# Tokenizer, state-space scan and expert layer on one core: taps, token means and expert products of the last stage issued at other steps

## The chip, the cores and the metric

One core of one Trainium2 chip runs the whole program. Times are device microseconds (us) of one execution; the time of a kernel is the median of its runs. About 0.2% (18 us) is what a measurement of this kernel can tell from no change.

## What is computed

A batch of 4 images (3 x 224 x 224) goes through two "performer" blocks that make tokens, and a projection makes 3136 tokens of 768 channels each. Then comes one layer: a state-space scan and a routed expert layer, each on a normalised input and added to it.

```python
t = _unfold3(t, 2).transpose(0, 2, 1)
h = t @ proj_w.T + proj_b                         # 3x3 taps, stride 2, of 64 channels
x = layernorm(h)
Bproj, Cproj = x @ W_B + b_B, x @ W_C + b_C       # 16 each
delta = softplus(x @ W_D + b_D + p_Delta)
state = exp(delta * A) * state + B_bar * x        # 768 x 16 states, token by token
h = h + sum_n(C[n] * state[n])
x = layernorm(h)
route = argmax(softmax((x @ enc_w + enc_b) @ sw_w + sw_b))          # one of 8 experts
h = h + prob * (gelu(x @ w1[route] + b1[route]) @ w2[route] + b2[route])
```

## The kernel before

Three stages follow each other: `performer1`, `performer2` and `tail`. Only `tail`, the last, is touched; it takes the span from about 3600 us on.

**Units and steps.** `tail` works on 28 units (`UNITS`) of 448 tokens (`T`; 4 images of 7 units). A unit has 24 steps (`STEPS`), one for each pair of a chunk of 128 channels (`dc`, 6 of them) and a group of 4 of the 16 states (`q`). In a step GpSimd (POOL) multiplies h by B (`weigh_in`, line 1482), ScalarE (ACT) makes four decays in PSUM (`step`, line 1762), VectorE (DVE) weighs with them (`weigh`, line 1871; four) and scans (`scan`, line 1880; two), GpSimd multiplies the states by C (`weigh_out`, line 1494, two steps later), and TensorE (PE) sums the states into bank YB (`step`, line 1573). After every fourth step an identity product adds h (line 1577), and ScalarE writes the result back to h (`add_to_h`, line 1751) one full step group later: at steps 3 (of the unit before), 7, 11, 15, 19 and 23. The v buffers form a ring of 6.

**Side work.** Between the steps stand two other chains. `front(i + 1, k)` makes the next unit's h and its B, C and delta: the taps, six products of 128 channels (lines 1532 and 1534, here PJ0 to PJ5), each moved out by ScalarE (line 1688, HW0 to HW5) before the next may start, since all use bank BF; a seventh tap product for the token means (MU, written by line 1691); sums of squares in two parts (VAR0, VAR1, line 1523); Ln and Exp of the variance (lines 1700 and 1702); the B and C product (BC) and the delta product (Z), both line 1527; and on VectorE the writes of B and C (lines 1852 to 1855), Z (1846) and delta (1861). `mlp(i - 1, k)` is the expert layer of the unit before: squares (SQ0, SQ1) and mean (MEAN) on TensorE, the encoder product (ENC), four expert products (IN0 to IN3, line 1527, each moved from bank BS by VectorE in line 1924 before the next may start), the route logits (LOG), the turned route (TURN, line 1609, copied by VectorE in line 1951, here OH), four masks (lines 1622 and 1957), and eight outputs (OUT0 to OUT7, lines 1635 to 1638), two banks in turn, each moved by ScalarE (line 1796).

**Order.** Every engine runs its own list in order: for step k of loop i first its part of the step, then `mlp(i - 1, k)`, then `front(i + 1, k)`. The steps at which each piece is issued are tuples of constants (from line 1330): P_ for TensorE, A_ for ScalarE, V_ for VectorE. The number in the tuple is a step of that engine's own list, and the engines are not at the same step at the same time: at every fourth step TensorE waits for an h write that stands in ScalarE's list three steps later (lines 1565 and 1751). The SyncE queue issues the loads and the spreads (lines 1346 to 1467); the token load of unit i + 2 (line 1358) waits until the seven tap products of unit i + 1 are done, the load of `w2` (line 1451) for IN3.

Of the kernel before, what the change touches and what calls it, by code (L numbers as in the profile page):

```python
# [42 lines left out]
def after(eng, s, count):  # L43

    if count > 0:
        eng.wait_ge(s, count)
# [1110 lines left out]
STEPS = Q * DC  # L1157
UNITS = B * J3
# [18 lines left out]
def tail(nc, sem, w, c, t2, w1c, xd, dd, bcd, out):  # L1177

    with ExitStack() as ctx:
# [5 lines left out]
        def bank(k, n=T, rows=slice(0, 128)):  # L1185
            return ps[rows, k, 0:n]
# [140 lines left out]
        s_oa = sem("t_out_written")  # L1327
        s_out = [sem("t_out_stored_even"), sem("t_out_stored_odd")]

        P_PJ, P_MU, P_VAR, P_Z, P_BC = 1, 7, (8, 10), 11, 9  # L1330
        A_HW, A_MU, A_SQ, A_RS, A_MX, A_SP = 5, 11, (9, 13), 14, (16, 17), (17, 18)
        V_Z, V_BC, V_DL = 15, 14, (18, 19)
        P_SQ, P_MEAN, P_ENC, P_IN, P_LOG, P_TURN = (0, 2), 1, 4, 5, 6, 10
        P_MASK, P_OUT = (12, 13, 14, 15), (16, 17, 18, 18, 19, 20, 21, 22)
        A_SQ2, A_MS, A_RS2, A_EX, A_GL = (2, 4), 5, 7, 11, 14
        A_OUT = (21, 22, 23, 23, 24, 25, 26, 27)
        V_VAR, V_ENC, V_IN, V_LOG, V_EQ, V_OH, V_MASK = 6, 8, 9, 10, 12, 14, (16, 17, 18, 19)
        ROUTE, TAIL = 9, 28

        def means(i):  # L1340

# [175 lines left out]
        def _(pe):  # L1517
            mm = nc.tensor.matmul

            def squares_sum(i, ln, into, chunks):  # L1520
                for dc in chunks:
                    pe.wait_ge(s_sq[ln], DC * i + dc + 1)
                    mm(into, jm[:, :], sq[:, dc % 3, :], start=(dc == 0), stop=(dc == DC - 1)).then_inc(s_var[ln], 1)  # L1523

            def over_chunks(into, weights, i):
                for dc in range(DC):
                    last = mm(into, weights(dc), h[:, i % 3, dc, :], start=(dc == 0), stop=(dc == DC - 1))  # L1527
                return last

            def taps(into, even, odd):  # L1530
                for j in range(3):
                    mm(into, even(j), x3[:, 0:TR3, j:j + 2 * S3 - 1:2], start=(j == 0), stop=False)  # L1532
                for j in range(3):
                    last = mm(into, odd(j), x3[0:64, 1:TR3 + 1, j:j + 2 * S3 - 1:2], start=False, stop=(j == 2))  # L1534
                last.then_inc(s_pj, 1)

            def front(i, k):
                if P_PJ <= k < P_PJ + DC:
                    dc = k - P_PJ
                    cols = slice(128 * dc, 128 * dc + 128)  # L1540
                    if dc == 0:
                        pe.wait_ge(s_x, 32 * (i + 1))
                        after(pe, s_dl, DC * i)
                    else:
                        pe.wait_ge(s_hw, DC * i + dc)
                    taps(bank(BF), lambda j: wpa[:, j, cols], lambda j: wpj[:, j, cols])
                if k == P_MU:
                    pe.wait_ge(s_hw, DC * (i + 1))
                    taps(ps[few, BF, 0:T], lambda j: wma[:, j, :], lambda j: wmb[:, j, :])
                if k == P_VAR[0]:  # L1550
                    pe.wait_ge(s_mu, i + 1)
                    squares_sum(i, 0, bank(BF), range(0, 3))
                if k == P_VAR[1]:
                    squares_sum(i, 0, bank(BF), range(3, DC))
                if k == P_Z:
                    pe.wait_ge(s_ln[0], i + 1)
                    over_chunks(bank(BF), lambda dc: wz[:, dc, :], i).then_inc(s_z, 1)
                if k == P_BC:
                    after(pe, s_he, MT * (i - 1))
                    over_chunks(ps[0:48, BS, 0:T], lambda dc: wbc[:, dc, :], i).then_inc(s_bc, 1)  # L1560

            def step(i, k):

                dc, q = divmod(k, Q)
                n = STEPS * i + k
                if q == 0:
                    after(pe, s_hy, DC * i + dc)
                if k in OWN:
                    pe.wait_ge(s_cv, 2 * owned(n))
                else:  # L1570
                    pe.wait_ge(s_cm, others(n))
                for g in range(4):
                    last = mm(ps[32 * g:32 * g + 32, YB, 0:T], dg[:, 4 * k + g, :], v[:, n % RING, g, 1:T + 1],  # L1573
                              start=(q == 0), stop=False)
                last.then_inc(s_ns, 1)
                if q == Q - 1:
                    mm(bank(YB), ident[:, :], h[:, i % 3, dc, :], start=False, stop=True).then_inc(s_hs, 1)  # L1577
# [74 lines left out]
            last.then_inc(s_pm, 1)  # L1652
            pe.wait_ge(s_dgm, 1)
            pe.wait_ge(s_pd, 16)
            for k in range(STEPS):
                front(0, k)
            for i in range(UNITS + 1):
                for k in range(TAIL if i == UNITS else STEPS):
                    if i < UNITS:
                        step(i, k)  # L1660
                    if i >= 2 and k + STEPS < TAIL:
                        mlp(i - 2, k + STEPS)
                    if i >= 1:
                        mlp(i - 1, k)
                    if i + 1 < UNITS:
                        front(i + 1, k)

        @block.scalar
        def _(act):
# [95 lines left out]
            def mlp(i, k):  # L1765
# [23 lines left out]
                for o in range(2 * NCH):  # L1789
                    if A_OUT[o] != k:  # L1790
                        continue
# [214 lines left out]
def build(nc, w, c, out):  # L2006
    t1 = nc.dram_tensor("tokens1", (B, E, T1ROWS, IMG), F32, kind="Internal").ap()
    t2 = nc.dram_tensor("tokens2", (B, E, T2ROWS, S2), F32, kind="Internal").ap()
    w1c = nc.dram_tensor("centred_w1", (128, DC, NX * NR), F32, kind="Internal").ap()
    xd = nc.dram_tensor("h_by_channel", (2, DC, 32, 4, T), F32, kind="Internal").ap()  # L2010
    dd = nc.dram_tensor("delta_by_channel", (2, DC, 32, 4, T), F32, kind="Internal").ap()
    bcd = nc.dram_tensor("bc_rows", (2, 2, N, T), F32, kind="Internal").ap()
    stages = (lambda sem: performer1(nc, sem, w["x"], w, c, t1),
              lambda sem: performer2(nc, sem, w, c, t1, t2),
              lambda sem: tail(nc, sem, w, c, t2, w1c, xd, dd, bcd, out))
    for stage in stages:
        sems = []

        def sem(name):
            sems.append(nc.alloc_semaphore(name))  # L2020
            return sems[-1]

        stage(sem)
        nc.clear_and_free_semaphores(sems)
        nc.all_engine_barrier()
# [133 lines left out]
```

## Time and profile before

| | before |
|---|---|
| median of 3 runs | 9070.57 us (9055.2 to 9074.09) |
| the profiled execution | 9071.86 us |
| its span, first to last instruction | 9070.1 us |
| mean granted TensorE clock | 0.916 |
| busy PE / DVE / ACT / POOL | 85% / 68% / 47% / 66% of the span |
| steps x units in the last stage | 24 x 28 |

The profile shows one execution. Busy shares are over all three stages; in the last stage POOL and DVE are busy nearly all the time. A row of a timeline gives start, duration, engine, line, operation, operands and count, and in brackets how long the engine had been idle and who released it. A duration of merged instructions runs from the first start to the last end; matmul ends are modelled, so the work of a piece is best read from one start to the next.

### The profile page before, as it was taken

How to read it: one execution, taken by the hardware profiler on the slowest of the kernel's cores; microseconds unless marked ns; L12 is line 12 of the kernel's file. 1: busy time of each engine (PE TensorE's matmuls, PEld its weight loads, DVE VectorE, ACT ScalarE, POOL GpSimd, SP SyncE). 2: the span in 40 equal slices, each digit the busy share in tenths (PEclk: the TensorE clock that was granted, in tenths of full speed). 3: DMA queues.
4: the chain of work that ended last, by engine and by line, in shares of the span. 5: the costliest groups of instructions: out<-in, count | busy, mean ns of one | idle time of the engine just before them, and what ended most of it. 6: DMA issues, size and time to landing. Idle time of an engine off the chain costs nothing.

```text
span 9070.1 us, 86859 instructions
## 1 busy us (share of the span) xinstructions
PE 7693.1 (85%) x31228; PEld 3214.3 (35%) x31228; DVE 6124.9 (68%) x6499; ACT 4306.6 (47%) x7641; POOL 5969.4 (66%) x2484
## 2 busy tenths in 40 slices
PE   6799999776999996588788888788887888888887
PEld 3444444322444432133333333333333333333333
DVE  1355555442233333988888888888888888888885
ACT  1366666553344432445544445444445444454442
POOL 0011111115766640998999989999989999899995
PEclk9999999998999997799889998899988899988988
DMA  0011111114544432223233223333232332233331
GB/s 26 22 41 45 39 44 41 31 31 83 104 100 100 99 65 68 95 98 119 96 120 115 100 96 119 106 112 116 94 119 96 123 112 100 99 116 106 117 110 50
DMA packets 356855, 786.60 MB, mean 87 GB/s; under 512 B 70437, under 2 KB 282806, under 8 KB 348936
## 3 DMA queue, kind: packets, MB, share of 16 engines
q1 hardware_dynamic: 320376, 690.75, 25.0%
q0 software_dynamic: 21712, 51.75, 2.2%
q10 hardware_dynamic: 14336, 38.54, 1.2%
q8 instruction: 247, 4.05, 0.2%
q14 instruction: 184, 1.51, 0.1%
HBM read 597.36 MB, written 183.35 MB: 86 GB/s over the span
## 4 chain that ended last, share of the span: by engine, by line
PE 34%; DVE 14%; ACT 5%; issue 5%; POOL 2%; DMA 0%; SPq 0%; DVEq 0%; ACTq 0%; POOLq 0%
PE ps L1527 7%; DVE v L1880 6%; PE ps L1635 6%; DVE v L1871 6%; PE ps L1534 5%; PE ps L1532 5%; PE ps L1573 3%; ACT ps L1762 3%; PE ps L1523 2%; PE ps L1638 2%; PE ps L1636 2%; PE ps L1577 1%; POOL v L1482 1%; POOL v L1494 1%; DVE dl L1861 1%
## 5 line engine op out<-in xcount | busy, mean ns | idle before, releaser
L1880 DVE TENSOR_TENSOR_SCAN v<-ps,v 128x898 f32<-128x898 f32 x1344 | 2725.5, 2028 | 92.4
L1494 POOL TENSOR_TENSOR v<-v,ct 128x1792 f32<-128x1792 f32 x672 | 2473.8, 3681 | 447.6 <-ACT st L1723 447.6
L1482 POOL TENSOR_TENSOR v<-xr,bt 128x1792 f32<-128x1792 f32 x672 | 2472.8, 3680 | 97.3 <-DMA xr<-h_by_channel 97.3
L1762 ACT ACTIVATE ps<-dr,aa 128x448 f32<-128x448 f32 x2688 | 1585.6, 627 | 1526.7 <-DVE v L1880 1509.5
L1871 DVE SCALAR_TENSOR_TENSOR v<-ps,aa,v 128x448 f32<-128x448 f32 x2688 | 1690.5, 671 | 553.6 <-ACT ps L1762 527.1
L222 POOL DMA_DIRECT2D tokens<-ob x448 | 235.4, 532 | 1878.2 <-ACT ob L383 1827.4
L1635 PE MATMUL ps<-w_or_w,gm 128*112 128x384 f32 x1792 | 719.9, 551 | 370.1 <-DVE gm L1957 277.5
L1573 PE MATMUL ps<-v,dg 128*32 128x448 f32 x5376 | 705.8, 599 | 206.9 <-POOL v L1494 106.3
L1635 PEld LDWEIGHTS ps<-w_or_w,gm 128*112 128x112 f32 x1792 | 334.0, 197 | 768.7 <-DVE gm L1957 319.9
L1527 PE MATMUL ps<-h,w_or_w 128*128 128x448 f32 x1344 | 536.8, 549 | 16.3 <-DVE gm L1924 16.3
L1532 PE MATMUL ps<-x,wpa 128*128 128x448 f32 x1008 | 445.3, 577 | 17.2 <-ACT h L1688 10.2
L1688 ACT ACTIVATE h<-ps,pbias 128x448 f32<-128x448 f32 x168 | 106.4, 633 | 732.7 <-PE ps L1534 732.7
L1534 PE MATMUL ps<-x,wpb 64*128 64x448 f32 x1008 | 448.3, 576 | 0.0
L498 DVE COPY ht<-ps 112x512 f32<-112x512 f32 x112 | 77.5, 692 | 546.6 <-ACT kp L411 546.6
L812 PE MATMUL ps<-xt,wa 128*64 128x448 f32 x2016 | 434.5, 564 | 0.0
L1523 PE MATMUL ps<-sq,jm 128*128 128x448 f32 x672 | 315.5, 611 | 61.5 <-ACT ot L1796 56.8
L1527 PEld LDWEIGHTS ps<-h,w_or_w 128*128 128x128 f32 x1344 | 250.3, 191 | 298.6 <-issue 279.2
L471 DVE RECIPROCAL qpn<-qpn 128x448 f32<-128x448 f32 x112 | 330.7, 2953 | 3.8
L1573 PEld LDWEIGHTS ps<-v,dg 128*32 128x32 f32 x5376 | 110.0, 112 | 611.2 <-issue 284.7
L1622 PE MATMUL ps<-wpb 9*128 9x448 f32 x224 | 151.8, 768 | 194.8 <-DVE gm L1957 194.1
L1118 DVE TENSOR_TENSOR kq<-ps,rsa 128x896 f32<-128x896 f32 x56 | 61.1, 1092 | 358.2 <-PE ps L820 336.9
L276 PE MATMUL ps<-wki,h 128*112 128x256 f32 x896 | 282.0, 398 | 21.3 <-DVE hu L493 21.3
(324 smaller groups left out, 11919.9 us busy)
## 6 DMA issues: line engine op xcount, KB each, us to landing
xr<-h_by_channel SPq DMA_DIRECT2D x168, 896.0 KB, 7.3
dr<-delta_by_channel SPq DMA_DIRECT2D x168, 896.0 KB, 6.3
x<-tokens SPq DMA_DIRECT2D x252, 224.0 KB, 5.3
tokens<-ob POOLq DMA_DIRECT2D x448, 112.0 KB, 2.4
w_or_w<-in_w SPq DMA_DIRECT2D x29, 1536.0 KB, 6.4
w_or_w<-centred_w SPq DMA_DIRECT2D x27, 1536.0 KB, 6.4
h_by_channel<-h SPq DMA_DIRECT2D x112, 336.0 KB, 10.9
delta_by_channel<-dl SPq DMA_DIRECT2D x112, 336.0 KB, 4.8
```

The source lines that it names most:

```text
L812: mm(ps[half[g], o, 0:T], wa[:, j, cols], xt[:, 2 * (n % 3) + g, 0:TR2, j:j + 2 * S2 - 1:2], start=(j == 0), stop=False)
L1482: tt(v[:, n % RING, :, 1:T + 1], xr[:, dc % 2, 1:].rearrange("p (i t) -> p i t", i=4), bt[:, q:q + 1, :].to_broadcast([128, 4, T]), ALU.mu ...
L1494: tt(v[:, n % RING, :, 1:T + 1], v[:, n % RING, :, 1:T + 1], ct[:, q:q + 1, :].to_broadcast([128, 4, T]), ALU.mult).then_inc(s_cm, 1)
L1523: mm(into, jm[:, :], sq[:, dc % 3, :], start=(dc == 0), stop=(dc == DC - 1)).then_inc(s_var[ln], 1)
L1527: last = mm(into, weights(dc), h[:, i % 3, dc, :], start=(dc == 0), stop=(dc == DC - 1))
L1532: mm(into, even(j), x3[:, 0:TR3, j:j + 2 * S3 - 1:2], start=(j == 0), stop=False)
L1534: last = mm(into, odd(j), x3[0:64, 1:TR3 + 1, j:j + 2 * S3 - 1:2], start=False, stop=(j == 2))
L1573: last = mm(ps[32 * g:32 * g + 32, YB, 0:T], dg[:, 4 * k + g, :], v[:, n % RING, g, 1:T + 1], start=(q == 0), stop=False)
L1635: mm(into[:, 0:D // 2], gm[:, m, cs], w2[:, m, lo:lo + D // 2], start=(m == 0), stop=False)
L1762: fn(decay(g), dr[:, dc % 2, g, :], ACT.Exp, scale=aa[:, 4 * k + g:4 * k + g + 1]).then_inc(s_a, 1)
L1871: stt(row, decay(g), aa[:, 4 * k + g:4 * k + g + 1], row, ALU.subtract, ALU.mult).then_inc(s_wt, 1)
L1880: nc.vector.tensor_tensor_scan(row, flat[:, 1024 * pair:1024 * pair + 2 * T + 2], row, 0.0, ALU.mult, ALU.add).then_inc(s_sc, 1)
```

## The change

The constants change, and TensorE's loops call the taps of a unit two steps before the first step of the loop in which they stood. P_PJ goes from 1 to -2: PJ0 and PJ1 are issued at steps 22 and 23 of the loop before, PJ2 to PJ5 at steps 0 to 3. ScalarE's HW0 to HW5 go from steps 5 to 10 to steps 2 to 7. MU, the squares, BC, the expert products, TURN's copy, the masks and the last outputs move by one or two steps. The last loop has 27 steps instead of 28 (`TAIL`). No instruction is added or removed.

```diff
-        P_PJ, P_MU, P_VAR, P_Z, P_BC = 1, 7, (8, 10), 11, 9
-        A_HW, A_MU, A_SQ, A_RS, A_MX, A_SP = 5, 11, (9, 13), 14, (16, 17), (17, 18)
+        P_PJ, P_MU, P_VAR, P_Z, P_BC = -2, 5, (7, 9), 11, 10
+        A_HW, A_MU, A_SQ, A_RS, A_MX, A_SP = 2, 9, (7, 11), 13, (16, 17), (17, 18)
         V_Z, V_BC, V_DL = 15, 14, (18, 19)
-        P_SQ, P_MEAN, P_ENC, P_IN, P_LOG, P_TURN = (0, 2), 1, 4, 5, 6, 10
-        P_MASK, P_OUT = (12, 13, 14, 15), (16, 17, 18, 18, 19, 20, 21, 22)
+        P_SQ, P_MEAN, P_ENC, P_IN, P_LOG, P_TURN = (0, 2), 1, 4, 6, 6, 10
+        P_MASK, P_OUT = (11, 12, 13, 14), (16, 17, 18, 18, 19, 20, 20, 21)
         A_SQ2, A_MS, A_RS2, A_EX, A_GL = (2, 4), 5, 7, 11, 14
-        A_OUT = (21, 22, 23, 23, 24, 25, 26, 27)
-        V_VAR, V_ENC, V_IN, V_LOG, V_EQ, V_OH, V_MASK = 6, 8, 9, 10, 12, 14, (16, 17, 18, 19)
-        ROUTE, TAIL = 9, 28
+        A_OUT = (21, 22, 23, 23, 24, 25, 25, 26)
+        V_VAR, V_ENC, V_IN, V_LOG, V_EQ, V_OH, V_MASK = 6, 8, 10, 10, 12, 13, (15, 16, 17, 18)
+        ROUTE, TAIL = 9, 27
...
-            for k in range(STEPS):
+            for k in range(P_PJ, STEPS):
                 front(0, k)
+            for k in range(P_PJ, 0):
+                front(1, k)
             for i in range(UNITS + 1):
                 for k in range(TAIL if i == UNITS else STEPS):
...
                     if i + 1 < UNITS:
                         front(i + 1, k)
+                    if i + 2 < UNITS and k >= STEPS + P_PJ:
+                        front(i + 2, k - STEPS)
```

## Rows read from the trace of the kernel before

**Rows 1.** The page's costliest groups: GpSimd's work on the states.

```profile
L1494 POOL TENSOR_TENSOR v<-v,ct 128x1792 f32<-128x1792 f32 x672 | 2473.8, 3681 | 447.6 <-ACT st L1723 447.6
```

**Rows 2.** Who waited for whom, 4000 to 8900 us: total, times, longest.

```profile
ACT h L1688 <- PE ps L1534: 667.8, 140, 7.5
DVE v L1871 <- ACT ps L1762: 504.8, 160, 4.8
POOL v L1494 <- ACT st L1723: 425.3, 201, 5.0
```

**Rows 3.** Timeline of DVE, 6700 to 6800 us: its waits at steps 7, 9 to 12, 14.

```profile
6727.62 1.27 DVE L1871 SCALAR_TENSOR_TENSOR v<-ps,aa,v 128x448 f32<-128x448 f32 x2 [2.93 <-ACT ps L1762]
...
6743.44 1.28 DVE L1871 SCALAR_TENSOR_TENSOR v<-ps,aa,v 128x448 f32<-128x448 f32 x2 [2.00 <-ACT ps L1762]
...
6755.44 1.28 DVE L1871 SCALAR_TENSOR_TENSOR v<-ps,aa,v 128x448 f32<-128x448 f32 x2 [4.84 <-ACT ps L1762]
...
6767.46 1.28 DVE L1871 SCALAR_TENSOR_TENSOR v<-ps,aa,v 128x448 f32<-128x448 f32 x2 [4.30 <-ACT ps L1762]
...
6777.18 1.28 DVE L1871 SCALAR_TENSOR_TENSOR v<-ps,aa,v 128x448 f32<-128x448 f32 x2 [2.56 <-ACT ps L1762]
...
6799.45 0.62 DVE L1852 TENSOR_TENSOR ps<-ps,rs 48x448 f32<-48x448 f32 x1 [0.42 <-ACT rs L1702]
```

**Rows 4.** Timeline of PE, OUT4 of one unit to MU of the next.

```profile
6673.22 2.83 PE L1635 MATMUL ps<-w_or_w,gm 128*112 128x384 f32 x8 [3.43 <-ACT ot L1796]
...
6677.65 0.96 PE L1573 MATMUL ps<-v,dg 128*32 128x448 f32 x8
...
6682.97 0.96 PE L1573 MATMUL ps<-v,dg 128*32 128x448 f32 x8
...
6699.66 4.85 PE L1523 MATMUL ps<-sq,jm 128*128 128x448 f32 x6 [2.56 <-ACT ot L1796]
...
6715.51 0.96 PE L1573 MATMUL ps<-v,dg 128*32 128x448 f32 x8
...
6723.85 0.96 PE L1573 MATMUL ps<-v,dg 128*32 128x448 f32 x8
...
6725.59 2.56 PE L1532 MATMUL ps<-x,wpa 128*128 128x448 f32 x6
...
6730.68 0.96 PE L1573 MATMUL ps<-v,dg 128*32 128x448 f32 x8
...
6741.42 0.96 PE L1573 MATMUL ps<-v,dg 128*32 128x448 f32 x8
...
6752.02 0.96 PE L1573 MATMUL ps<-v,dg 128*32 128x448 f32 x8
...
6775.03 0.96 PE L1573 MATMUL ps<-v,dg 128*32 128x448 f32 x8
```

**Rows 5.** Timeline of PE further on: TURN, Z after an idle stretch, the next OUT4.

```profile
6789.82 0.93 PE L1609 MATMUL ps<-ident,eq 112*9 112x112 f32 x8
...
6798.86 7.52 PE L1527 MATMUL ps<-h,wz 128*128 128x448 f32 x12 [3.82 <-ACT rs L1700]
...
6865.09 4.53 PE L1635 MATMUL ps<-w_or_w,gm 128*112 128x384 f32 x8 [3.43 <-ACT ot L1796]
...
6871.22 0.96 PE L1573 MATMUL ps<-v,dg 128*32 128x448 f32 x8
```

**Rows 6.** Timeline of ACT, 6700 to 6800 us: HW4 and its wait.

```profile
6752.13 0.63 ACT L1688 ACTIVATE h<-ps,pbias 128x448 f32<-128x448 f32 x1 [7.54 <-PE ps L1534]
```

**Rows 7.** Timeline of DVE: the first scans of steps 21 and 22.

```profile
6848.28 2.03 DVE L1880 TENSOR_TENSOR_SCAN v<-ps,v 128x898 f32<-128x898 f32 x1
...
6854.81 2.03 DVE L1880 TENSOR_TENSOR_SCAN v<-ps,v 128x898 f32<-128x898 f32 x1
```

**Rows 8.** Groups of DVE instructions, 3900 to 8900 us: the moves of IN0 to IN3.

```profile
L1924 DVE TENSOR_TENSOR gm<-ps,rs2t 128x448 f32<-128x448 f32 x105 | 63.0, 600 | 1.2 <-PE ps L1527 1.2
```

**Rows 9.** Stretch of Z: busy time and count of PE, PEld, DVE, ACT, POOL; clock, DMA.

```profile
6798.90:6806.30 7.40, 7.40 (x12) 3.31 (x12) 6.74 (x10) 4.67 (x11) 5.91 (x3) 0.63 0.37 132
```

## The prediction

> **What bounds the kernel now.** I read the costliest groups first. GpSimd's two products are 3.68 us each, two a step and 24 steps, so 176.7 us of work a unit, and it is idle only because ScalarE's copy of the last states is late [rows 1]. The table of waits says who makes it late: GpSimd waits for ScalarE, ScalarE's h writes (HW) wait for TensorE's taps, and VectorE then waits for ScalarE's decays [rows 2]. The timeline of VectorE shows where in a unit: 2.93 us at step 7, 2.00, 4.84, 4.30 and 2.56 at steps 9 to 12 [rows 3]. It never waits for GpSimd in this unit, so it is VectorE's work plus these waits that make the unit's length.
>
> The timeline of TensorE gives the cycle that closes on itself. One period runs from OUT4 (released by ScalarE) at 6673.22 to the next OUT4 at 6865.09, 191.87 us [rows 4, 5]. It has three parts: (a) TensorE's row of pieces from OUT4 to the end of MU at 6775.03, 101.81 us, nearly without idle time; (b) from there by ScalarE to VectorE's step 12 at 6777.18 [rows 3], 2.15 us; (c) VectorE's steps 12 to 22 and the hand-over to OUT4, 87.91 us. In (a) ScalarE's in-order list keeps VectorE at TensorE's pace. So the change must be judged by where TensorE's row ends and how many steps VectorE then still has to do.
>
> **Part (a), after.** The last piece that ScalarE waits for is now PJ5, issued at step 3 and moved out at step 7; MU, at step 5, is wanted only at ScalarE's step 9. From starts to next starts in [rows 4]: an output 4.43; a step's sum and an output 5.32, so a sum 0.89; a sum with the identity product 1.74; a tap product 5.09; sum, squares and taps 8.34; sum, twelve matmuls of a full product and taps 10.60. The new row is
> - OUT4 4.43, sum and OUT5 5.32, OUT6 4.43, sum and OUT7 5.32: 19.50;
> - step 22: sum and PJ0, 5.98; step 23: sum, identity, PJ1, 6.83;
> - step 0: SQ0 and PJ2, 8.34; step 1: MEAN and PJ3, 10.60; step 2: SQ1 and PJ4, 8.34; step 3: sum, identity, PJ5, 6.83.
>
> That is 66.42 us. OUT4 follows 3.43 us of idle time, and the second OUT4 took 6.13 to its next start, 1.70 more [rows 5]; I take this for every unit, so 68.1. Against 101.81, 33.7 go: ENC, three IN, LOG, MU and the sums of four steps, and with them SQ0's 2.56 us wait for ScalarE's last output move [rows 4], because OUT7 now comes ahead of the taps.
>
> The price is seen inside the row: the identity product of step 23, which ScalarE needs for its h write at step 3 before any decay, now stands behind PJ0. So VectorE gets a new wait at step 3, and others at 5, 6 and 7. They are not added: TensorE's row holds them all.
>
> **Part (b), after.** The h write of PJ5 is followed by three squares, as HW4 is now: TensorE done at 6752.02, VectorE going on at 6755.44 [rows 3, 4, 6], 3.4 us, 1.3 more than MU's.
>
> **Part (c), after.** It starts at step 8 instead of 12. Four steps of 6.53 (6848.28 to 6854.81) [rows 7] are 26.1. The side work of VectorE that moves into this part is ENC, LOG's three small operations and a net three of the IN moves: five pieces of about 0.6 each [rows 8], 3.0. The rest of the side work is the same, a step earlier or later; it is never on a path of its own.
>
> The IN chain becomes a round trip: TensorE is now on time, so IN1 waits for VectorE's move of IN0 at step 10, after some 4 us of idle time. From that move TensorE does IN1 4.62, VAR0 2.36, twice a sum with a product 5.51, VAR1 2.36, a sum 0.89 and TURN 0.86 (6789.82 to the next piece, estimated from its 0.93) [rows 4, 5], 22.1 us. VectorE does three steps 19.6, three IN moves 1.8, LOG 0.6 and the route's small operations, estimated at 1.1: 23.1. Then it wants TURN for OH, at step 13 now and not 14. At the full clock that is no wait. But Z, after 3.82 us idle, took 7.52 us where such a product takes 4.6, with a mean granted clock of 0.63 in its stretch, between the levels of 1.2 and 2.4 GHz [rows 5, 9]. The same after IN1's idle time adds 1.7 (OUT4's excess) to 2.9 (Z's). I take 2.3, so OH waits 1.3 us; the ends are 0.7 and 1.9. ScalarE's Ln waits for VAR1 too and adds 0.2 behind it; the 0.42 us wait at step 14 [rows 3] goes, since Ln and Exp are now a step earlier.
>
> By a rule of the Trainium skill it would be worse. "TensorE: Matmul & The Clock Gate", Part 1, says that back-to-back matmuls at the lower clock start twice as far apart. Were IN1 so throughout, it would add 4.6 and not 2.3; the trace has 2.9 at most. This is a rival below.
>
> **Costed at nothing.** Masks and OUT0, OUT1 come one step earlier, but OUT2 and OUT3 wait for ScalarE's moves of steps 21 and 22, so the wait at step 23 stays. BC goes behind TURN, hidden before VectorE's step 14. The eighth output's move at step 2 waits for OUT7 on ScalarE, and so do its squares and HW0; VectorE feels it only through the same h write at step 3. On the SyncE queue the token load comes earlier and is not needed for 12 steps; `w2` waits for IN3, a step later, and holds back the spread for chunk 4, with a few us left before GpSimd wants it and a ring of 6 behind that. GpSimd, at 176.7 us, has room under 189. The last loop's missing step holds no work.
>
> **The sum.** 68.1 + 3.4 + 87.9 + 26.1 + 3.0 + 1.3 + 0.2 - 0.4 = 189.6 against 191.87: 2.3 us less a unit. Loops 1 to 26 have both chains: 26 x 2.3 = 60. The profiled execution took 9071.86; 9012, and the median is 1.3 under that execution: **9011 us**. It is the difference of two large numbers, 33.7 off TensorE's row and 31 put back elsewhere, so an error of 2 us in either moves the total by 52.
>
> **Rivals.**
> - *The waits simply go.* If the taps, being early, held nobody up, the five waits, 16.6 us a unit, would vanish, down to GpSimd's 176.7: 26 x 15.2 = 395 less, 8675. For it: these waits are by name the taps'. Against it: TensorE's row has no idle time in it to give. 5%.
> - *The row stays warm.* If neither OUT4 nor IN1 meets the lower clock, 1.7 + 1.3 more go, 5.3 a unit: 8933. For it: TensorE is busier ahead of OUT4 in some units (6673.22 was at full clock). 14%.
> - *Nothing gained.* IN1 wholly at the lower clock: OH waits 3.6 instead of 1.3, which eats the 2.3: 9071. 14%.
> - *Slower.* Place: step 13, OH behind TURN. If the lower clock lasts over IN1 and VAR0, it adds 7.0, OH waits 6.0, 4.7 more than I took: 2.4 a unit lost, 26 times, 9133. It decides from an excess of 4.6 us. For it: a new gap, new lower-clock work on the path, and VAR0 directly behind. Against it: in none of the rows did it last so long under load. 22%.
>
> That the change does not do what it says is not in doubt: constants and calls match.
>
> **How the numbers follow.** My case has 45%. The range, 8930 to 9135, reaches from the warm row to the slower rival; outside it are the first rival and a part of the last. A measurement of this kernel can tell about 0.2%, 18 us, from no change. Faster: 45 + 5 + 14 = 64%; same 14%; slower 22%.
>
> **What would show it.** VectorE's waits at steps 9 to 12 gone, new ones at step 3 (4 to 6 us) and 5 to 7 (some 8 together); step 23's wait still near 4; TensorE's row from OUT4 to PJ5's end at 66 to 69; IN1 released by line 1924 after idle time; a wait of VectorE of 1 to 2 us at line 1951 or its step. GpSimd idle near 13 a unit. I am wrong if the row is longer than 71, if OH waits over 3.6, or if VectorE waits for GpSimd's line 1482.

## The result and the profile after

| | before, beside it | after |
|---|---|---|
| median | 9070.36 us (4 runs) | 9103.71 us (4 runs, 9094.68 to 9111.47) |
| ratio, 95% interval | | 1.003 [1.0017, 1.0042] |
| the profiled execution, its span | 9071.86, 9070.1 us | 9098.96, 9097.2 us |
| mean granted clock | 0.916 | 0.911 |

The change makes the kernel slower, by 33 us in the medians and by 0.3% in the ratio, more than the 0.2% that a measurement can tell. The forecast was 9011 us, faster; its range, 8930 to 9135, held the result. Now and then an execution of any of these kernels takes far longer (12353.83 us in one of the four of pjm1), and such executions are left out of the ratios and of pjm1's median.

VectorE after, from step 3 of a unit to step 23, in the timeline (start, duration, engine, line, operation, count, idle time before and releaser). Line numbers of ScalarE and VectorE are 4 higher than before, those of TensorE up to 1638 the same: the weighing is L1875 now, the move of an expert product L1928, the copy of the route L1955.

```profile
6727.76 1.28 DVE L1875 SCALAR_TENSOR_TENSOR v<-ps,aa,v 128x448 f32<-128x448 f32 x2 [6.66 <-ACT ps L1766]
...
6741.19 1.28 DVE L1875 SCALAR_TENSOR_TENSOR v<-ps,aa,v 128x448 f32<-128x448 f32 x2 [0.26 <-ACT ps L1766]
...
6751.79 1.28 DVE L1875 SCALAR_TENSOR_TENSOR v<-ps,aa,v 128x448 f32<-128x448 f32 x2 [3.96 <-ACT ps L1766]
...
6761.88 1.28 DVE L1875 SCALAR_TENSOR_TENSOR v<-ps,aa,v 128x448 f32<-128x448 f32 x2 [2.93 <-ACT ps L1766]
...
6768.43 1.25 DVE L1875 SCALAR_TENSOR_TENSOR v<-ps,aa,v 128x448 f32<-128x448 f32 x2
...
6788.82 0.60 DVE L1928 TENSOR_TENSOR gm<-ps,rs2t 128x448 f32<-128x448 f32 x1
...
6800.54 1.28 DVE L1875 SCALAR_TENSOR_TENSOR v<-ps,aa,v 128x448 f32<-128x448 f32 x2 [3.50 <-ACT ps L1766]
...
6817.95 0.62 DVE L1955 TENSOR_TENSOR wpb<-ps,mu 9x448 f32<-9x448 f32 x1 [2.24 <-PE ps L1609]
6818.82 1.28 DVE L1875 SCALAR_TENSOR_TENSOR v<-ps,aa,v 128x448 f32<-128x448 f32 x2 [0.24 <-ACT ps L1766]
...
6889.42 1.28 DVE L1875 SCALAR_TENSOR_TENSOR v<-ps,aa,v 128x448 f32<-128x448 f32 x2 [3.45 <-ACT ps L1766]
```

The waits of [rows 3] at steps 9, 10 and 11 are gone. New ones stand at steps 3, 5, 6 and 7 (6.66, 0.26, 3.96, 2.93), and the one at step 23 stayed (3.45): all these were forecast. The row without a bracket, 6768.43, is the first weighing of step 8. What was not forecast is the wait of 3.50 us **at step 12**, and the 2.24 at step 13 is larger than the 1.3 I had put there.

TensorE in the same unit:

```profile
6695.84 5.46 PE L1635 MATMUL ps<-w_or_w,gm 128*112 128x384 f32 x8 [3.43 <-ACT ot L1800]
...
6764.94 0.96 PE L1573 MATMUL ps<-v,dg 128*32 128x448 f32 x8
...
6783.63 1.02 PE L1577 MATMUL ps<-h,ident 128*128 128x448 f32 x2
6789.47 6.86 PE L1527 MATMUL ps<-h,w_or_w 128*128 128x448 f32 x12 [4.83 <-DVE gm L1928]
6796.17 2.42 PE L1523 MATMUL ps<-sq,jm 128*128 128x448 f32 x6
...
6807.74 6.26 PE L1527 MATMUL ps<-h,w_or_w 128*128 128x448 f32 x12 [2.67 <-DVE gm L1928]
...
6890.99 2.83 PE L1635 MATMUL ps<-w_or_w,gm 128*112 128x384 f32 x8 [3.43 <-ACT ot L1800]
```

The row from OUT4 (6695.84) to PJ5's end (6764.94) is 69.10 us long; in [rows 4] the row to MU's end was 101.81. IN1 (6789.47) waits for VectorE's move of IN0, and VAR0 (6796.17) stands behind it. IN3 (6807.74) waits in the same way for the move of IN2, at VectorE's step 12, and VAR1 and TURN stand behind it. ScalarE shows who stands behind VAR0: the second squares of the front, L1684, and later Ln, L1704, behind VAR1.

```profile
6797.18 0.58 ACT L1684 ACTIVATE sq<-h 128x448 f32<-128x448 f32 x1 [6.84 <-PE ps L1523]
...
6816.30 0.63 ACT L1704 ACTIVATE rs<-ps,eps 128x448 f32<-128x448 f32 x1 [7.76 <-PE ps L1523]
```

The table of waits of after, 4000 to 8900 us (total, times, longest), says that this happens in each of the 25 units of the stretch:

```profile
DVE v L1875 <- ACT ps L1766: 502.3, 187, 7.0
ACT h L1692 <- PE ps L1534: 458.5, 150, 5.3
POOL v L1494 <- ACT st L1727: 451.0, 222, 4.4
...
ACT rs L1704 <- PE ps L1523: 176.2, 25, 7.8
ACT sq L1684 <- PE ps L1523: 172.6, 75, 6.8
```

Against [rows 2], ScalarE waits less for the taps (667.8 before, 458.5 now), VectorE as long for ScalarE (504.8, 502.3), GpSimd longer (425.3, 451.0). The last two rows are waits that [rows 2] do not show.

**The sum, redone with this unit.** Unit length is 6890.99 - 6695.84 = 195.15. Part (a) 69.10, forecast 68.1. Part (b), 6764.94 to 6768.43, 3.49, forecast 3.4. Part (c), 6768.43 to 6890.99, 122.56; forecast 87.9 + 26.1 + 3.0 + 1.3 + 0.2 - 0.4 = 118.1. The 4.46 that are over in (c) are the wait at step 12 (3.50) and 0.98 more at step 13 and behind it (2.24 + 0.24 against 1.3 + 0.2): 4.48. The sum needs nothing else; what stands behind the 2.24 is taken up with the reasons below.

In the next unit OUT4 met the full clock, and that unit took 190.55: 2.77 less in (a), waits of 2.89 and 0.76 in place of 3.50 and 2.24. The units go on in that beat, and the mean of the 26 units that have both chains, from VectorE's first weighing of one to that of the next, is 192.8 (before 191.8, by the same count). The forecast 189.6 plus the mean wait at step 12, 3.2, is 192.8.

### The profile page after: what moved, and what is told of

The parts are those of the page before. It is cut to its first block, busy times and chain, and to the rows that moved or that the text cites. A ratio compares the mean times of both kernels' runs of the same rounds, so it can differ in the third digit from the quotient of the medians.

```text
span 9097.2 us, 86859 instructions
## 1 busy us (share of the span) xinstructions
PE 7754.3 (85%) x31228; PEld 3257.6 (36%) x31228; DVE 6124.5 (67%) x6499; ACT 4320.2 (47%) x7641; POOL 5968.6 (66%) x2484
## 4 chain that ended last, share of the span: by engine, by line
PE 28%; DVE 19%; issue 7%; ACT 4%; POOL 3%; DMA 0%; SPq 0%; DVEq 0%; ACTq 0%; POOLq 0%
DVE v L1884 8%; DVE v L1875 8%; PE ps L1635 6%; PE ps L1527 5%; PE ps L1534 4%; PE ps L1532 4%; PE ps L1523 3%; ACT ps L1766 2%; PE ps L1573 2%; PE ps L1638 2%; POOL v L1482 2%; PE ps L1636 2%; POOL v L1494 1%; DVE dl L1865 1%; PE ps L1577 1%
## 5 line engine op out<-in xcount | busy, mean ns | idle before, releaser
L1494 POOL TENSOR_TENSOR v<-v,ct 128x1792 f32<-128x1792 f32 x672 | 2470.0, 3676 | 463.2 <-ACT st L1727 463.2
L1875 DVE SCALAR_TENSOR_TENSOR v<-ps,aa,v 128x448 f32<-128x448 f32 x2688 | 1691.3, 671 | 543.6 <-ACT ps L1766 516.0
L1635 PE MATMUL ps<-w_or_w,gm 128*112 128x384 f32 x1792 | 785.3, 592 | 281.5 <-ACT ot L1800 241.9
L1527 PE MATMUL ps<-h,w_or_w 128*128 128x448 f32 x1344 | 607.4, 607 | 206.0 <-DVE gm L1928 206.0
L1635 PEld LDWEIGHTS ps<-w_or_w,gm 128*112 128x112 f32 x1792 | 362.5, 213 | 691.1 <-ACT ot L1800 313.2
L1527 PEld LDWEIGHTS ps<-h,w_or_w 128*128 128x128 f32 x1344 | 278.4, 215 | 537.7 <-issue 288.3
L747 POOL TENSOR_TENSOR css<-xs 128x560 f32<-128x560 f32 x112 | 125.1, 1117 | 252.6 <-ACT xs L952 252.5
```

Source lines behind the costliest of these rows:

```text
L1494: tt(v[:, n % RING, :, 1:T + 1], v[:, n % RING, :, 1:T + 1], ct[:, q:q + 1, :].to_broadcast([128, 4, T]), ALU.mult).then_inc(s_cm, 1)
L1635: mm(into[:, 0:D // 2], gm[:, m, cs], w2[:, m, lo:lo + D // 2], start=(m == 0), stop=False)
L1875: stt(row, decay(g), aa[:, 4 * k + g:4 * k + g + 1], row, ALU.subtract, ALU.mult).then_inc(s_wt, 1)
```

## The experiments

Each run's time is set beside runs of the kernel before that were taken on the same chip at the same time. "Unused matmuls" are matmuls whose result nobody reads.

### The wait at step 12

My theory after the result: the second squares stand in ScalarE's list at step 11 now, and wait for VAR0, which stands in TensorE's list behind IN1's round trip; VectorE's decays of step 12 are behind them. Rivals: the lower clock on IN1 (the mechanism of two rivals of the prediction), or OH, VectorE's copy of the route.

**v6**: VAR0 a step earlier, so ahead of IN1.

```diff
-        P_PJ, P_MU, P_VAR, P_Z, P_BC = -2, 5, (7, 9), 11, 10
+        P_PJ, P_MU, P_VAR, P_Z, P_BC = -2, 5, (6, 9), 11, 10
```

> The changed kernel with VAR0 (the first three sums of squares) issued at TensorE's step 6, ahead of the wait for IN0's move, instead of step 7 behind IN1. Theory (squares): in the changed kernel ScalarE's second squares stand at its step 11 and wait for VAR0, which stands behind IN1's round trip, so VectorE waits 3.2 us at step 12 of each unit. With VAR0 ahead, that wait goes, and TURN comes earlier as well, so VectorE's 1.5 us wait for OH goes too: 3.2 to 4.7 us less in each of 26 units, 8980 to 9020 us, faster than the kernel before. Rival (clock): the surplus over my sum is TensorE's lower clock after idle stretches; then moving VAR0 changes little, 9080 to 9110.

Measured: 9026.33 us against 9067.9, ratio 0.9943 [0.9929, 0.9958]. The waits of L1684 for L1523 are not among the waits any more, and VectorE has none at step 12; a unit takes 189.8. This is the largest single part of what the forecast missed. The time is 6 us above the range of the theory: OH still waits 0.76 us in every unit, behind IN3, and OUT4 now meets the lower clock in every unit (its first eight matmuls take 4.5 to 5.5 us, where after has 5.5 and 2.8 in turn).

**sq13**: the squares go back to step 13, where before had them; TensorE's list is that of after.

```diff
-        A_HW, A_MU, A_SQ, A_RS, A_MX, A_SP = 2, 9, (7, 11), 13, (16, 17), (17, 18)
+        A_HW, A_MU, A_SQ, A_RS, A_MX, A_SP = 2, 9, (7, 13), 13, (16, 17), (17, 18)
```

> The changed kernel with ScalarE's second squares of the front at step 13, as before the change, instead of step 11. Theory (squares): ScalarE no longer stands at VAR0, the 3.2 us wait at step 12 goes, while the wait for OH stays at 1.3 to 2: 3.2 less in each of 26 units, about 9020. Rival (clock): 9080 to 9110, since no work of TensorE has moved.

Measured: 9053.43 against 9067.9, 0.9978 [0.9968, 0.9987], some 50 us less than after and 33 more than expected. It changes ScalarE's list alone, and the wait at step 12 becomes 0.64 us, now of the move of IN1 itself, IN1 being late:

```profile
6782.52 0.63 DVE L1928 TENSOR_TENSOR gm<-ps,rs2t 128x448 f32<-128x448 f32 x1 [0.64 <-PE ps L1527]
...
6792.03 0.62 DVE L1955 TENSOR_TENSOR wpb<-ps,mu 9x448 f32<-9x448 f32 x1 [0.87 <-PE ps L1609]
```

Of the size of these 33 us is what OUT4 costs: its first eight matmuls take 5.5 us in each of the 26 units, 4.1 in the mean in after, so 1.4 more a unit or 35 us in all. So the edit changed the place of the lower clock too, and not the order alone.

**fill**: 12 unused matmuls ahead of IN1, so that TensorE is not idle before it; nothing else changes.

```diff
                     else:
+                        if m == 1:
+                            pe.wait_ge(s_mu, min(i + 3, UNITS))
+                            over_chunks(bank(BF), lambda dc: jm[:, :], i)
                         pe.wait_ge(s_he, MT * i + m)
```

> The changed kernel with twelve more matmuls (a product whose result is not used) at TensorE's step 7, in the idle stretch ahead of IN1, so that IN1 runs at the full clock. Theory (squares): VAR0 comes 2 us earlier, so the wait at step 12 shrinks from 3.2 to about 1.2 and is not gone: 2 to 3 less a unit, 9025 to 9055. Rival (clock): the whole surplus of 3.3 a unit and the OH wait go, 8975 to 9015. If the clock has no part: 9100 or slower.

Measured: 9071.13 against 9067.9, 1.0003 [0.9993, 1.0012], slower than either theory had it. TensorE's timeline in fill: the unused product, IN1, VAR0.

```profile
6764.64 4.67 PE L1527 MATMUL ps<-h,jm 128*128 128x448 f32 x12
6769.62 4.78 PE L1527 MATMUL ps<-h,w_or_w 128*128 128x448 f32 x12 [0.31 <-DVE gm L1931]
6774.24 2.42 PE L1523 MATMUL ps<-sq,jm 128*128 128x448 f32 x6
```

IN1 takes 4.78 here and 6.86 in after. The lower clock on it was real: without it the kernel gains some 25 to 30 us, though OUT4 now meets the lower clock in four units of five instead of every second, which takes back some 20. But VectorE still waits 1.4 us at step 12 and 1.5 at step 13 in the mean. So the clock enlarges the wait; the order makes it.

**oh14**: VectorE's copy of the route a step later, where before had it.

```diff
-        V_VAR, V_ENC, V_IN, V_LOG, V_EQ, V_OH, V_MASK = 6, 8, 10, 10, 12, 13, (15, 16, 17, 18)
+        V_VAR, V_ENC, V_IN, V_LOG, V_EQ, V_OH, V_MASK = 6, 8, 10, 10, 12, 14, (15, 16, 17, 18)
```

> The changed kernel with VectorE's copy of the turned route (OH) at step 14 instead of 13. I counted its wait, 1.5 us a unit, as a cost. Theory (two waits side by side): ScalarE's Ln of the variance waits for VAR1 at the same place, which holds the decays of step 14 until almost the same time; so moving OH alone gives less than 0.6 us a unit, 9090 to 9105. Rival (OH alone is the cost): 1.5 a unit goes, 9065.

Measured: 9159.38 against 9067.9, 1.0089 [1.0072, 1.0106], 0.6% worse than after, where I had expected a small gain. VectorE in oh14, steps 12 and 14:

```profile
6643.47 1.28 DVE L1875 SCALAR_TENSOR_TENSOR v<-ps,aa,v 128x448 f32<-128x448 f32 x2 [3.31 <-ACT ps L1766]
...
6661.65 1.28 DVE L1875 SCALAR_TENSOR_TENSOR v<-ps,aa,v 128x448 f32<-128x448 f32 x2 [3.01 <-ACT ps L1766]
```

The wait at step 12 stays, and step 14 gets one of 3.01, released by ScalarE: Ln stands in ScalarE's list at step 13, and waits there for VAR1. So OH was not alone at step 13: two waits for TensorE's same row lay over each other, and taking one away bared the other. I had put only 0.2 us on Ln. In both kernels step 14 begins 2.63 us after TensorE is done with VAR1 (6816.19 to 6818.82 in after, 6659.02 to 6661.65 here). After has its 2.24 us of OH, OH's own 0.62 of work and the 0.24 of step 14 inside that time, 3.1 together; here the 0.62 are done later and the whole is wait. The kernel becomes slower by this, and by the lower clock: IN3 takes 6.0 us or more here in every unit and in after in every second one (0.8 a unit in the mean), and the wait at step 3 is 0.6 longer.

### Both variance parts ahead of the next expert product

**v68**: VAR0 ahead of IN1 and VAR1 ahead of IN3.

```diff
-        P_PJ, P_MU, P_VAR, P_Z, P_BC = -2, 5, (7, 9), 11, 10
+        P_PJ, P_MU, P_VAR, P_Z, P_BC = -2, 5, (6, 8), 11, 10
```

> The kernel of the run before last thought (VAR0 at TensorE's step 6) with VAR1 at step 8 as well, instead of 9, so ahead of IN3. Theory: with VAR0 alone moved, VectorE still waited 0.76 us at OH and 0.25 at step 14 of each unit, and oh14 showed that it is ScalarE's Ln behind VAR1 that holds step 14, not OH. With both parts of the squares ahead of the next round trip, both waits go: about 1.0 less a unit than with VAR0 alone, 26 less, near 9000. Rival: these two waits are covered by the others, no change against the 9026 with VAR0 alone (9015 to 9035).

Measured: 8978.38 against 9081.02, 0.9883 [0.9869, 0.9898]. VectorE in v68, from step 7 of a unit to its step 23 (the waits of steps 3, 5 and 6 are the ones of after, 6.66, 0.26 and 3.96).

```profile
6692.59 1.28 DVE L1875 SCALAR_TENSOR_TENSOR v<-ps,aa,v 128x448 f32<-128x448 f32 x2 [2.92 <-ACT ps L1766]
...
6742.87 0.62 DVE L1955 TENSOR_TENSOR wpb<-ps,mu 9x448 f32<-9x448 f32 x1
...
6814.12 1.27 DVE L1875 SCALAR_TENSOR_TENSOR v<-ps,aa,v 128x448 f32<-128x448 f32 x2 [3.45 <-ACT ps L1766]
```

The copy of the route (6742.87) has no wait left, nor has step 12. The unit is 188.2 in the mean. By the forecast's own sum without its OH and Ln terms it would be 189.6 - 1.3 - 0.2 = 188.1. One tuple stands between the change as made, 0.3% slower, and one that is 1.2% faster.

**keep**: v68 with 6 unused matmul pairs before OUT2 and 4 before OUT4, to keep OUT4 off the lower clock.

```diff
+                    if o == 2 or o == 4:
+                        pe.wait_ge(s_dl, DC * min(i + 3, UNITS))
+                        for _ in range(6 if o == 2 else 4):
+                            mm(bank(BF), jm[:, :], rs2[:, :], start=True, stop=True)
                     if o >= 2:
```

> As v68, and with matmuls whose result is not used ahead of TensorE's waits for OUT2 (6) and OUT4 (4), where it is idle for 5 and 3.4 us. With VAR0 moved, OUT4 took 7.2 us in every unit where it takes 4.5 at the full clock, and TensorE's row from OUT4 to PJ5 is all on the path. Theory: the lower clock at OUT4 is worth its whole excess, 2.7 a unit: 60 to 75 under v68, near 8930. Rival: the added matmuls themselves push OUT4 back, or the clock falls all the same: no gain or slower than v68.

Measured: 8975.84 against 9081.02, 0.9899 [0.9865, 0.9934]; v68 is inside that interval. The 60 to 75 us of the theory did not come: three of the four executions took 8971.28 to 8975.97, and v68's took 8965.3 to 8983.95. OUT4's first eight matmuls took 2.9 us in every unit of the profile, so the edit did what it should; why it gained nothing is open. The profiled execution is the fourth (9041.4 us, granted clock 0.890), in which a full product took 4.8 us throughout and not 4.6, so its rows can't be set against v68's.

**pjm1**: v68 with the taps begun one step ahead and not two.

```diff
-        P_PJ, P_MU, P_VAR, P_Z, P_BC = -2, 5, (6, 8), 11, 10
-        A_HW, A_MU, A_SQ, A_RS, A_MX, A_SP = 2, 9, (7, 11), 13, (16, 17), (17, 18)
+        P_PJ, P_MU, P_VAR, P_Z, P_BC = -1, 5, (6, 8), 11, 10
+        A_HW, A_MU, A_SQ, A_RS, A_MX, A_SP = 3, 9, (7, 11), 13, (16, 17), (17, 18)
```

> As v68, with the taps one step later (PJ0 at TensorE's step 23, behind the identity product, HW0 at ScalarE's step 3). Theory (the sum of rows): the 6.5 us wait at step 3, behind PJ0, shrinks to 1 to 2, but PJ5 is issued at step 4 behind ENC and ends 5.6 us later, and VectorE goes on from step 9 and not 8: in sum 1 to 2 less a unit, 25 to 50 under v68. Rival (the wait at step 3 is a cost of its own): all of its 5 us goes, 130 under v68. If it is slower than v68, the row's reckoning is wrong.

Measured: 8971.46 (3 executions) against 9081.02, 0.9885 [0.9866, 0.9905], the same as v68; neither theory's gain came. The waits stand elsewhere (0.9 us at step 3 in place of some 6.1, but 2.0 at step 9, 2.2 at step 11 and 0.9 at step 13 besides the 3.8 and 2.9 at steps 6 and 7), and their sum is 16.7 a unit against 16.9. So to begin the taps two steps ahead and not one buys nothing.

### The change in its two halves

**taps**: the taps two steps ahead, as in after, with the loops' calls for them; all other constants as before.

```diff
-        P_PJ, P_MU, P_VAR, P_Z, P_BC = -2, 5, (7, 9), 11, 10
-        A_HW, A_MU, A_SQ, A_RS, A_MX, A_SP = 2, 9, (7, 11), 13, (16, 17), (17, 18)
+        P_PJ, P_MU, P_VAR, P_Z, P_BC = -2, 7, (8, 10), 11, 9
+        A_HW, A_MU, A_SQ, A_RS, A_MX, A_SP = 2, 11, (9, 13), 14, (16, 17), (17, 18)
```

> The changed kernel's taps alone: PJ0 to PJ5 three steps earlier and their moves at ScalarE's steps 2 to 7, all else as before the change, so MU stays at step 7 behind IN2. Theory: the row from OUT4 to PJ5 is as short as in the changed kernel, but MU, behind IN2 and its round trip, is now the last piece that ScalarE waits for at step 11, and holds VectorE 3 to 4 us at step 12; there is no wait at OH: 0 to 1 less a unit than before, 9050 to 9085. Rival (the taps carry the gain of v68): 8970 to 9000.

Measured: 9162.69 against 9082.55, 1.0085 [1.007, 1.01], 80 us slower, outside the ranges of theory and rival. VectorE in taps, steps 3, 7 and 11, and TensorE's IN1:

```profile
6761.10 1.28 DVE L1875 SCALAR_TENSOR_TENSOR v<-ps,aa,v 128x448 f32<-128x448 f32 x2 [6.19 <-ACT ps L1766]
...
6795.22 1.28 DVE L1875 SCALAR_TENSOR_TENSOR v<-ps,aa,v 128x448 f32<-128x448 f32 x2 [2.93 <-ACT ps L1766]
...
6816.29 6.32 PE L1527 MATMUL ps<-h,w_or_w 128*128 128x448 f32 x12 [5.91 <-DVE gm L1928]
...
6827.19 1.28 DVE L1875 SCALAR_TENSOR_TENSOR v<-ps,aa,v 128x448 f32<-128x448 f32 x2 [3.01 <-ACT ps L1766]
```

The waits at steps 3, 6 and 7 have come, and at steps 11 and 12 waits of 3.01 and 2.57 are left. The second is MU's, as the theory had it. The first it had missed: the identity product of TensorE's step 7, which ScalarE wants at its step 11, stands behind IN1, and IN1 is a round trip here (idle 5.91 us for VectorE's move of IN0, then 6.25 long). The sum of the waits is 23.0 a unit, before 20.5.

**rest**: the kernel before with the new constants of the expert layer alone: no early taps, and token means, variance and BC where they were.

```diff
-        P_SQ, P_MEAN, P_ENC, P_IN, P_LOG, P_TURN = (0, 2), 1, 4, 5, 6, 10
-        P_MASK, P_OUT = (12, 13, 14, 15), (16, 17, 18, 18, 19, 20, 21, 22)
+        P_SQ, P_MEAN, P_ENC, P_IN, P_LOG, P_TURN = (0, 2), 1, 4, 6, 6, 10
+        P_MASK, P_OUT = (11, 12, 13, 14), (16, 17, 18, 18, 19, 20, 20, 21)
...
-        V_VAR, V_ENC, V_IN, V_LOG, V_EQ, V_OH, V_MASK = 6, 8, 9, 10, 12, 14, (16, 17, 18, 19)
+        V_VAR, V_ENC, V_IN, V_LOG, V_EQ, V_OH, V_MASK = 6, 8, 10, 10, 12, 13, (15, 16, 17, 18)
...
```

> The change without its taps: the kernel before with only the constants of the expert layer and of the last outputs changed (IN0 to IN3, the copy of the turned route, the masks, OUT6 and OUT7), the taps and the front's other work as before. Theory: BC stands at TensorE's step 9 ahead of TURN and now waits for IN3's move at VectorE's step 13, just behind which VectorE wants TURN; so VectorE waits 6 to 7 us at OH, against some 2.6 saved at MU: 3 to 4.5 slower a unit, 9150 to 9190. Rival (parts are independent): the taps alone brought the loss, this is at or under 9070.

Measured: 9073.87 against 9081.02, 0.999 [0.9981, 1.0], where the theory had 9150 to 9190. TensorE in rest, IN3, BC and TURN:

```profile
6788.43 4.78 PE L1527 MATMUL ps<-h,w_or_w 128*128 128x448 f32 x12 [0.55 <-DVE gm L1924]
6796.45 6.06 PE L1527 MATMUL ps<-h,wbc 128*48 128x448 f32 x12 [3.24 <-DVE gm L1924]
...
6803.22 0.93 PE L1609 MATMUL ps<-ident,eq 112*9 112x112 f32 x8
```

VectorE in rest, its copy of the route:

```profile
6804.19 0.62 DVE L1951 TENSOR_TENSOR wpb<-ps,mu 9x448 f32<-9x448 f32 x1 [7.80 <-PE ps L1609]
```

BC needs the bank of IN3, waits for VectorE's move of it, and TURN, which needs none of this, stands behind BC in TensorE's list. VectorE waits 7.80 us at step 13 (8.0 in the mean) and gives back what it gained at steps 7, 9, 10, 14 and 23, which is 8.1 in the mean. The theory had the wait, but put what is saved at 2.6.

**rest10**: rest with BC behind TURN.

```diff
-        P_PJ, P_MU, P_VAR, P_Z, P_BC = 1, 7, (8, 10), 11, 9
+        P_PJ, P_MU, P_VAR, P_Z, P_BC = 1, 7, (8, 10), 11, 10
```

> The kernel of run rest (the change without its taps) with BC at TensorE's step 10, behind TURN, instead of step 9. In rest VectorE waited 8.04 us at OH in every unit, TURN standing behind BC, which waits for IN3's move at VectorE's step 13; its other waits had shrunk by about as much. Theory: with TURN ahead of BC the 8.04 us go and nothing takes their place but 0 to 2 us behind VAR1 or Z: 6 to 8 less a unit, 8865 to 8915, under v68, though the taps stand where they stood before the change. Rival (the row of TensorE only slips on): the 8 us appear at another wait of the same unit, 9050 to 9075.

Measured: 8891.08 us (8880.29 to 8896.27) against 9082.55, 0.9788 [0.9772, 0.9804]. This is the best of all versions, 2.1% faster than before and 2.3% faster than after by the medians (8891.08 / 9103.71). TensorE, OUT4 and the piece behind MU, then the next OUT4:

```profile
6573.22 5.42 PE L1635 MATMUL ps<-w_or_w,gm 128*112 128x384 f32 x8 [3.44 <-ACT ot L1796]
...
6667.35 0.96 PE L1573 MATMUL ps<-v,dg 128*32 128x448 f32 x8
...
6757.54 5.42 PE L1635 MATMUL ps<-w_or_w,gm 128*112 128x384 f32 x8 [3.43 <-ACT ot L1796]
```

and VectorE's step 12 and copy of the route:

```profile
6669.51 1.28 DVE L1871 SCALAR_TENSOR_TENSOR v<-ps,aa,v 128x448 f32<-128x448 f32 x2 [2.57 <-ACT ps L1762]
...
6684.71 0.62 DVE L1951 TENSOR_TENSOR wpb<-ps,mu 9x448 f32<-9x448 f32 x1
```

The same three parts as before: (a) 6573.22 to 6667.35 is 94.13 us against 101.81; (b) 2.16 against 2.15; (c) 6669.51 to 6757.54 is 88.03 against 87.91. The whole gain of the unit, 184.32 against 191.87, is in (a). One expert product fewer stands ahead of MU (its next start comes 4.60 later). SQ0's wait of 2.56 us [rows 4] is gone, as OUT7 is issued and moved a step earlier, and with the wait the lower clock behind it (rest has neither in its steady units, bc10 has both in every second or third): SQ0 took 4.78 us to the next start in [rows 4] and takes 2.45 here, and with the step's sum behind it that is 2.9. Against these stands OUT4, 7.90 us to the next output here and 5.32 in [rows 4]. Together these make 7.5 of the 7.7. GpSimd is idle 215.7 us ahead of its L1494 in the groups of the profile's page, where [rows 1] have 447.6, so some 8 us a unit are left above its own 176.7.

**bc10**: the kernel before with BC behind TURN, and nothing else (the diff is the same line as in rest10).

> before with the B and C product behind the route's turn (P_BC 9 to 10) and nothing else. Theory (in before the route is copied at VectorE's step 14, so BC ahead of TURN holds nobody there, and the waits at steps 9 to 12 come from pieces issued at TensorE's steps 5 to 7, ahead of both; the gain of rest10 needs the expert products a step later as well, and the order is only what stops the loss at step 13): no gain of note, 9050 to 9085. Rival (the gain of rest10 is the order by itself): 8885 to 8920.

Measured: 9080.21 against 9077.06, 1.0 [0.999, 1.001], as the theory had it. Each half of rest10 alone is worth nothing that can be measured (0.999 and 1.0), both together 2.1%: the later expert products shorten the row, and the order is what keeps the wait from coming back at step 13.

**early1**: rest10 with taps, token means and h writes one step earlier.

```diff
-        P_PJ, P_MU, P_VAR, P_Z, P_BC = 1, 7, (8, 10), 11, 10
-        A_HW, A_MU, A_SQ, A_RS, A_MX, A_SP = 5, 11, (9, 13), 14, (16, 17), (17, 18)
+        P_PJ, P_MU, P_VAR, P_Z, P_BC = 0, 6, (8, 10), 11, 10
+        A_HW, A_MU, A_SQ, A_RS, A_MX, A_SP = 4, 11, (9, 13), 14, (16, 17), (17, 18)
```

> rest10 with TensorE's row of the front one step earlier (PJ from step 0 instead of 1, token means at 6 instead of 7) and ScalarE's copy of the means at 4 instead of 5; variance, expert, B and C products where rest10 has them. Theory (a wait goes only where what the waiting engine needs was really moved ahead of a round trip, so the row from OUT4 to the means has to lose IN1's round trip for the waits at VectorE's steps 10 to 12 to go): MU stands ahead of IN1 and its wait, which took some 6.4 us with its sum and identity products; of the waits at VectorE's steps 11 and 12 (4.28 and 2.57 us in rest10) most goes, less 1 to 2 us that come back at steps 6 and 7: 4 to 6 us less for a unit, 8740 to 8790 us. Rival (the early row only carries the wait forward, as the taps alone did): waits of 5 to 7 us at VectorE's steps 3 to 7 in place of those at 11 and 12: 8870 to 8910 us.

Measured: 9060.5 (10 runs) against 9081.06, 0.9978 [0.9969, 0.9988]: 170 us worse than rest10, and outside what either theory gave. TensorE around step 7 in early1 (MU's second half, the sum, the identity product, IN1, and IN2 behind idle time):

```profile
6764.32 2.57 PE L1534 MATMUL ps<-x,wmb 64*9 64x448 f32 x6
6766.82 0.96 PE L1573 MATMUL ps<-v,dg 128*32 128x448 f32 x8
6767.71 1.02 PE L1577 MATMUL ps<-h,ident 128*128 128x448 f32 x2
6768.57 4.67 PE L1527 MATMUL ps<-h,w_or_w 128*128 128x448 f32 x12
...
6777.80 7.80 PE L1527 MATMUL ps<-h,w_or_w 128*128 128x448 f32 x12 [3.67 <-DVE gm L1924]
```

IN2 waits for VectorE's move of IN1. VectorE in early1, steps 11, 12, 13 and 15:

```profile
6770.59 1.28 DVE L1871 SCALAR_TENSOR_TENSOR v<-ps,aa,v 128x448 f32<-128x448 f32 x2 [4.11 <-ACT ps L1762]
...
6785.64 0.62 DVE L1924 TENSOR_TENSOR gm<-ps,rs2t 128x448 f32<-128x448 f32 x1 [1.35 <-PE ps L1527]
...
6795.15 0.62 DVE L1951 TENSOR_TENSOR wpb<-ps,mu 9x448 f32<-9x448 f32 x1 [0.86 <-PE ps L1609]
...
6805.90 1.28 DVE L1871 SCALAR_TENSOR_TENSOR v<-ps,aa,v 128x448 f32<-128x448 f32 x2 [1.53 <-ACT ps L1762]
```

MU is no longer the last hand-over, but now it stands **ahead** of the identity product of step 7, which ScalarE wants at its step 11. From OUT4 (6678.87) to that product's end (6768.57) the row is 89.70 us, 4.43 less than rest10's to MU; but VectorE has step 11 still to do, 7.1 us with the move in it, and IN2, behind 3.67 us of idle time and 7.80 us long, brings the waits of 1.35, 0.86 and 1.53 with it. That is 10.8 - 4.4 = 6.4 of the 6.8 us by which the unit is longer (191.15 against 184.32). Both theories of mine had looked only at the places where the waits had been.

## Why the prediction was wrong

Its mechanism, a cycle of TensorE's row, a hand-over by ScalarE and VectorE's remaining steps, held in every run that I read in this way; the row of 69.10 us, the waits and IN1's idle time came as it said, and none of its signs of being wrong did (VectorE waited for GpSimd's line 1482 for 1.2 us in the whole stretch). These parts of its sum were right to within a few tenths:

- Part (a): 66.42 at the full clock; measured 66.33 and 66.34 (69.10 and then the next unit's row, each without OUT4's excess). The excess of OUT4, 1.70 in every unit, was 2.77 in one and none in the next, in the mean 1.4. The list of what leaves the row was too short: SQ0's lower clock went with its wait, 2.9 us with the sum behind it. The row was counted from its own pieces, so 68.1 does not rest on that list.
- Part (b): 3.4; measured 3.49.
- The waits: step 3, 4 to 6, measured 5.6 in the mean (6.66 and 4.51 in turn); steps 5 to 7, some 8, measured 7.15; step 23, near 4, measured 3.45 and 3.74. Those at steps 9 to 11 went.
- IN1 behind idle time: released by VectorE's move after 4.83 us, forecast 4. Its excess over 4.62 was 2.1 and 1.5 in turn, forecast 2.3.

**The step that failed** is the last sentence of part (c): "The rest of the side work is the same, a step earlier or later; it is never on a path of its own." One piece of it was on a path. The front's second squares went from ScalarE's step 13 to 11, and VAR0, which frees their tile, stood in TensorE's list behind IN1, which the same paragraphs had just made a round trip through VectorE's step 10. I had written that chain down as the way to TURN, and had followed it to OH only, not to each of its readers on the way. v6 moves VAR0 and the wait of 3.2 us a unit goes; sq13 moves the squares and it goes but for 0.64.

The second fault is in the same chain, and there the number came out by luck. OH's wait was 2.24 and 0.76 in turn, 1.5 in the mean against 1.3. But the chain that I had counted has one round trip, IN1's, and there are two: IN3 waits 2.67 us for VectorE's move of IN2 and then takes 6.10 to its next start, not 4.62. From IN1's start to the start behind TURN (6789.47 to 6817.84) TensorE needs 28.4 us and not 22.1 + 2.3; VectorE needs 26.3 from its move of IN0 to OH and not 23.1, as the wait at step 12 is in it. The two errors nearly cancel. "At the full clock that is no wait" is wrong as well: in the units of fill in which IN1 and IN3 both take 4.61, OH waits 0.76. And oh14 shows that ScalarE's Ln, behind VAR1, holds VectorE as long as OH does; I had counted 0.2.

The **slower rival** (22%) came out on the right side, but not by its mechanism: it wanted an excess of over 4.6 us at IN1, and 2.1 were there. In fill, without that excess, the kernel is still not faster than before. The range held the result by luck: its upper end is this rival's time. **Nothing gained**, the rival by the page "TensorE: Matmul & The Clock Gate" of the Trainium skill (Part 1), wanted IN1 at twice its length. It took 6.70 to the next start against 4.62, with a granted clock of 0.68 over the stretch (second row: length, then busy time and count of PE, PEld, DVE, ACT, POOL, clock, DMA):

```profile
6695.84:6703.90 8.06, 8.06 (x24) 3.58 (x24) 7.92 (x7) 3.64 (x9) 8.06 (x3) 0.65 0.74 243
6789.40:6796.20 6.80, 6.73 (x13) 3.34 (x14) 6.59 (x10) 0.94 (x4) 6.80 (x3) 0.68 0.00 0
...
6890.99:6896.30 5.31, 5.31 (x24) 2.46 (x24) 5.28 (x5) 1.94 (x5) 5.31 (x2) 1.00 0.85 267
6699.66:6705.80 6.14, 6.13 (x15) 2.06 (x15) 6.00 (x7) 2.76 (x7) 6.14 (x2) 0.53 0.94 360
```

So a part of IN1 ran at the lower level (1.2 GHz) and the rest at the upper (2.4 GHz). The first and third row are OUT4 in two successive units. The last row is from the kernel before, SQ0 and the sum behind it: a granted clock of 0.53, and SQ0 took 4.78 us to its next start (4.85 in [rows 4]) against 2.36 for VAR0. There the trace agrees with the page, a whole piece twice as long; at IN1 the lower clock did not last that long.

**The waits simply go** (5%) fell: the taps' waits moved forward and did not vanish.

What I did not consider is that the two halves of the change could be judged apart. Early taps cost 0.85% alone; the later expert products with TURN ahead of BC are worth 2.1% alone. The change joins them, with MU and the variance earlier too (no run moves these alone), and adds the wait at step 12.

## What to carry to other kernels

When a piece is moved in a hand-written order, list for every instruction behind a new round trip who reads its result or waits for its buffer, on every engine, and at which step of that engine's own list; here the reader that stood earliest set the cost, not the one that comes last in the chain. Judge such a cycle by its rows: moving a hand-over pays only if it takes more off the row before it than the steps that are left behind it add, and each of the row's other hand-overs has to be priced in the same way. Try an order in its halves too, since two edits that are worth nothing alone can be worth 2% together, and a good one can hide behind a bad one.

## What the runs showed of the hardware

TensorE's lower clock can set a beat from unit to unit. In after, units of 195.2 and 190.5 us follow each other with hardly an exception: OUT4's stretch has a granted clock of 0.65 in one and 1.00 in the next, behind the same 3.43 us of idle time. IN3, behind the same 2.67 us, takes 6.10 us in one and 4.62 in the next. The kernel before has such a beat too: eleven times SQ0 takes 4.8 us behind 2.6 us of idle time, each time after an OUT4 at the full clock (2.8 us for its first eight matmuls); where OUT4 took 4.5 or 5.5, SQ0 waited 1.8 and took 2.5 to 4.2. In v6 the lengths of the units repeat every three units (190.6, 190.3, 189.2), in v68 mostly every five, and in rest10 there is no beat (184.3 to 184.4 in nearly all, OUT4 at the lower clock in each). A single row's excess is therefore not to be taken for the mean: the two units in [rows 4, 5] showed 0 and 1.70, after 2.77 and 0. How the phase passes from one unit to the next was not tried by itself.

Nor does the lower clock stay where it was when the order changes. Sq13 moves only pieces of ScalarE, and OUT4 meets the lower clock in every unit instead of every second, which costs 35 us. A busy TensorE ahead of a piece does bring it back: in fill IN1 takes 4.78 us and not 6.86.
